# Expert tiles in float32: the expert's weights become the moving operand, the GELU outputs are turned for the second product, and the high and low parts go

## The reference, cut to what matters

```
h2 = layernorm(x) * g + b                      # 2048 x 192
logits = h2 @ gate_w + gate_b                  # 8 experts
wts, sel = top_k(logits, 2); wts = softmax(wts)
for e in range(8):
    he  = gelu(h2 @ w1[e] + b1[e])             # 192 -> 768
    res = res + cw[:, e:e+1] * (he @ w2[e] + b2[e])   # 768 -> 192
```

## Time and profile before

| what | value |
|---|---|
| median of three runs | 1736.37 us |
| the profiled execution: span from first to last instruction | 1779.8 us |
| TensorE busy with matmuls | 1403.7 us (79%) |
| VectorE, ScalarE, GpSimd busy | 890.2, 471.8, 238.8 us |
| mean granted TensorE clock | 0.703 of full |
| the expert tiles on TensorE, from the first transposes to the last product | 930.7 to 1139.4 us |

### The profile page before, as it was taken

One profiled execution on the slowest core, in us unless ns is written; L12 is line 12 of the kernel. 1 busy time (PEld: TensorE's weight loads), 2 busy tenths in 40 slices (PEclk: granted clock), 3 DMA queues, 4 the chain that ended last, 5 costly groups with the idle time before them and its releaser, 6 DMA issues.

```text
span 1779.8 us, 44781 instructions
## 1 busy us (share of the span) xinstructions
PE 1403.7 (79%) x19314; PEld 1194.5 (67%) x19314; DVE 890.2 (50%) x2335; ACT 471.8 (27%) x878; POOL 238.8 (13%) x248
## 2 busy tenths in 40 slices
PE   6888888897879999999639999616689999986251
PEld 5868776887657777777537777415689898985131
DVE  4444545445445464342523333345366666664876
ACT  1221122112224342241323333114113333313130
POOL 4100000004022000000160000252322222200000
PEclk9767877877679796595559999857555555555565
DMA  8000000012021000000131111110000000000001
GB/s 291 1 18 18 18 0 18 18 35 62 1 81 42 2 2 2 1 2 2 50 111 32 39 39 37 47 47 1 3 4 3 3 3 3 3 3 1 1 0 36
DMA packets 28771, 48.07 MB, mean 27 GB/s; under 512 B 3632, under 2 KB 21696, under 8 KB 28352
## 3 DMA queue, kind: packets, MB, share of 16 engines
q1 hardware_dynamic: 25536, 39.33, 7.4%
q0 software_dynamic: 3072, 6.30, 1.2%
HBM read 33.20 MB, written 12.41 MB: 26 GB/s over the span
## 4 chain that ended last, share of the span: by engine, by line
PE 62%; DVE 19%; POOL 10%; ACT 6%; issue 3%; DMA 0%; POOLq 0%; ACTq 0%; DVEq 0%
PE ps L1117 8%; PE ps L1229 6%; PE ps L831 6%; PE ps L941 4%; PE ps L897 4%; PE ps L1132 4%; DVE big L507 3%; DVE big L512 3%; POOL big L766 3%; POOL big L770 3%; PE ps L1003 2%; PE ps L966 2%; PE ps L851 2%; PE ps L525 2%; PE ps L1277 2%
## 5 line engine op out<-in xcount | busy, mean ns | idle before, releaser
L1229 PE MATMUL ps<-big 128*128 128x2 bf16 x7680 | 222.3, 165 | 43.8 <-POOL big L770 20.8
L1229 PEld LDWEIGHTS ps<-big 128*128 128x128 bf16 x7680 | 215.0, 104 | 56.4 <-DVE big L1994 23.8
L1117 PE MATMUL ps<-big 128*128 128x128 bf16 x1170 | 141.6, 218 | 1.0 <-DVE big L1910 0.5
L525 PE MATMUL ps<-ident,big 128*128 128x128 f32 x384 | 86.4, 411 | 66.7 <-ACT big L519 66.7
L1117 PEld LDWEIGHTS ps<-big 128*128 x1170 | 111.7, 96 | 27.3 <-issue 2.4
L525 PEld LDWEIGHTS ps<-ident,big 128*128 128x128 f32 x384 | 74.1, 217 | 82.5 <-ACT big L519 82.5
L831 PE MATMUL ps<-consts,big 96*128 96x192 f32 x512 | 111.3, 382 | 12.1 <-POOL iota L695 12.1
L831 PEld LDWEIGHTS ps<-consts,big 96*128 96x128 f32 x512 | 107.5, 260 | 12.9 <-issue 12.1
L1982 DVE TENSOR_REDUCE big<-ps 128x24 f32<-128x48 f32 x160 | 32.8, 205 | 142.3 <-PE ps L1229 141.7
L1917 DVE TENSOR_TENSOR big<-big 128x512 bf16<-128x512 f32 x78 | 41.5, 558 | 103.5 <-ACT big L1511 103.1
L507 DVE TENSOR_REDUCE big<-ps 128x3 f32<-128x768 f32 x64 | 58.1, 949 | 61.2 <-PE ps L881 61.2
(11 more groups left out here) (360 smaller groups left out, 2595.4 us busy)
## 6 DMA issues: line engine op xcount, KB each, us to landing
big<-x_dram SPq DMA_DIRECT2D x16, 384.0 KB, 3.4
consts<-packed_dram SPq DMA_DIRECT2D x1, 4459.0 KB, 17.8
rows_dram<-big SPq DMA_DIRECT2D x1, 3744.0 KB, 18.1
big<-rows_dram SPq DMA_DIRECT2D x39, 96.0 KB, 2.0
results_dram<-big SPq DMA_DIRECT2D x39, 96.0 KB, 1.6
big<-w_dram SPq DMA_DIRECT2D x12, 288.0 KB, 3.7
big<-w_dram SPq DMA_DIRECT2D x16, 192.0 KB, 4.0
big<-w_dram SPq DMA_DIRECT2D x4, 576.0 KB, 6.0
```

The lines of the kernel that those rows point to most:

```text
L525: last = nc.tensor.transpose(ps[s][:, k // 4, (k % 4) * P:(k % 4 + 1) * P], bufs[s].p[:, k * P:(k + 1) * P], ident[:, :])
L1117: last = nc.tensor.matmul(ps[0][:, 2 * (i % 2) + m // 4, m % 4 * P:(m % 4 + 1) * P], e_at(expert, at, P), side, start=(k == 0), stop=(k == ...
L1229: last = nc.tensor.matmul(sums[:, 2 * k:2 * k + 2], kernel_part(i, part)[:, at:at + P], x_parts[g % 4][:, k, 0:2], start=(part == 0), stop ...
```

## The change

The split is gone: tokens, weights and hidden values stay float32, and TensorE multiplies them as such.

- `m_turn(i)`: two float32 transposes, each of 96 columns of the rows, into partitions 0 to 95.
- `m_up(i)`: the turned tokens are now stationary (96 or 97 rows by 128; row 96 is a row of ones that brings in the bias), and the expert's weights, still named by a register, move: 512 and then 256 columns, two products each, four in all. The result has the tokens on the partitions. It has one buffer (two PSUM banks), not two.
- ScalarE applies GELU once. The hidden values must then be turned: `m_turn_hidden(i)`, six float32 transposes, and VectorE copies them out (`m_heT`), two copies.
- `m_down(i)`: six products, with the turned hidden values stationary and 192 columns of weights moving. VectorE copies the result (`m_y`) where it added halves before.
- TensorE's loop is one step deeper: turn tile i + 2, up of tile i + 1, turn the hidden values of tile i, down of tile i - 1.
- An expert is loaded straight into its place by two DMAs: three at the very start, three once the first values of the second attention are there (`f_xn`), two after its end (`f_out`). GpSimd, ScalarE and VectorE split nothing. SyncE's loop over the tiles is as it was.

```
-                for m in range(HT):
-                    for k, side in enumerate(sides):
-                        at = k * HIDDEN + m * P
-                        last = nc.tensor.matmul(ps[0][:, 2 * (i % 2) + m // 4, m % 4 * P:(m % 4 + 1) * P],
-                                                e_at(expert, at, P), side, start=(k == 0), stop=(k == CHUNKS - 1))
+                for half, cols in enumerate(m_halves):
+                    if i >= 1:
+                        pe.wait_ge(sem("m_gelu"), 2 * (i - 1) + half + 1)
+                    for c in range(2):
+                        rows = HC + 1 - c
+                        last = nc.tensor.matmul(m_hidden(half), e_x[i % 2][0:rows, c * P:(c + 1) * P],
+                                                e_at(expert, rows, c * HIDDEN + cols.start, cols.stop - cols.start),
+                                                start=(c == 0), stop=(c == 1))
+            def m_turn_hidden(i):
+                for half, cols in enumerate(m_halves):
+                    if i >= 1:
+                        pe.wait_ge(sem("m_heT"), 2 * (i - 1) + half + 1)
+                    pe.wait_ge(sem("m_gelu"), 2 * i + half + 1)
+                    for at in range(cols.start, cols.stop, P):
+                        last = nc.tensor.transpose(m_turned_hidden(half)[:, at - cols.start:at - cols.start + P],
+                                                   e_he[i % 2][:, at:at + P], ident[:, :])
+                    last.then_inc(sem("m_hidden_turned"), 1)
...
-                    for part, n in ((e_hi, 2 * C), (e_lo, C)):
-                        last = nc.tensor.matmul(o[:, 0:n], part[i % 2][:, cols], e_at(expert, at, n),
+                    last = nc.tensor.matmul(m_y_out(i), e_heT[i % 2][:, m * P:(m + 1) * P],
+                                            e_at(expert, P, 2 * HIDDEN + m * C, C), start=(m == 0), stop=(m == HT - 1))
...
-            for i in range(-1, TILES):
+            for i in range(-1, TILES + 1):
...
                 if 0 <= i and i + 2 < TILES:
                     m_turn(i + 2)
                 if i + 1 < TILES:
-                    m_up(i + 1, expert)
-                if 0 <= i:
-                    m_down(i, older)
+                    m_up(i + 1, experts[i + 1])
+                if 0 <= i < TILES:
+                    m_turn_hidden(i)
+                if 1 <= i:
+                    m_down(i - 1, experts.pop(i - 1))
...
+            for i in range(TILES + 1):
+                if i + 2 < TILES:
+                    m_x(i + 2)
+                if i < TILES:
+                    m_heT(i)
+                if 1 <= i:
+                    m_y(i - 1)
```

More of the change, by code:

```diff
@@ L301, in build, with e_at @@
         TILES = 2 * T // P + EXPERTS - 1
[L302 to L329, removed]
+        W_WORDS = 2 * HIDDEN + HT * C
+        W_AT = X3_AT - EXPERTS * W_WORDS
+        EARLY = tuple(range(EXPERTS - 1, 1, -1))
+        LATE = (1, 0)
+        assert f_used[0] <= W_AT + EARLY[-1] * W_WORDS
+        e_all = big[:, W_AT:X3_AT].rearrange("p (e n) -> p e n", e=EXPERTS)
+        e_bytes = big[:, W_AT:X3_AT].bitcast(U8).rearrange("p (e n) -> p e n", e=EXPERTS)
+        def e_at(expert, rows, at, n):
+            return e_bytes[0:rows, bass.ds(expert, 1), 4 * at:4 * (at + n)].rearrange("p o n -> p (o n)").bitcast(F32)
         IN_TOK = 3
@@ L371, in turned_back, with m_hidden, m_x_out, m_turned_hidden @@
             return ps[bank // 4][:, bank % 4, 0:2 * C].rearrange("p (s c) -> p s c", s=2)
+        m_halves = (slice(0, 4 * P), slice(4 * P, HIDDEN))
+        def m_hidden(half):
+            return ps[0][:, half, 0:(4 - 2 * half) * P]
+        def m_x_out(i):
+            return ps[0][0:HC, 2 + i % 2, 0:2 * P]
+        def m_turned_hidden(half):
+            return ps[1][:, half, 0:(4 - 2 * half) * P]
+        def m_y_out(i):
+            return ps[1][:, 2 + i % 2, 0:C]
         def stores(k):
@@ L597, in _ @@
                         "o p c n -> (o p) c n")).then_inc(sem(f"tok_x{s}"), 16)
[L599 to L612, removed]
-            sp.wait_ge(sem("b1_stored"), 16)
[L614 to L619, removed]
+            sp.wait_ge(sem("f_xn"), 1)
+            for e in EARLY[IN_TOK:]:
+                load_expert(e)
+            sp.wait_ge(sem("f_out"), U)
+            for e in LATE:
+                load_expert(e)
+            sp.wait_ge(sem("b1_kept"), 1)
+            sp.dma_start(b1s, b1_rows).then_inc(sem("b1_stored"), 16)
+            sp.wait_ge(sem("b1_stored"), 16)
+            sp.dma_start(e_all[HC:HC + 1, :, 0:HIDDEN],
+                         b1s.rearrange("(o e m) n -> o e (m n)", o=1, e=EXPERTS)).then_inc(sem("b1_loaded"), 16)
             def load_rows(i):
@@ L1102, in m_turn @@
                     pe.wait_ge(sem("m_x"), i - 1)
-                o = ps[1][:, i % 2, 0:ROW // 2].bitcast(BF16)
-                for c in range(3):
-                    last = nc.tensor.transpose(o[:, c * P:(c + 1) * P], e_row[i % 4][:, c * P:(c + 1) * P], identb[:, :])
+                for c in range(2):
+                    last = nc.tensor.transpose(m_x_out(i)[:, c * P:(c + 1) * P],
+                                               e_row[i % 4][:, c * HC:(c + 1) * HC], ident[:, :])
                 last.then_inc(sem("m_turned"), 1)
@@ L1498, in _ @@
                                  ACT.Copy).then_inc(sem("moe_cwT"), 1)
-            late_hi(1)
-            late_hi(2)
             def m_gelu(i):
                 if i >= 2:
-                    act.wait_ge(sem("m_down"), i - 1)
-                for half, cols in enumerate((slice(0, 4 * P), slice(4 * P, HIDDEN))):
+                    act.wait_ge(sem("m_hidden_turned"), 2 * (i - 1))
+                for half, cols in enumerate(m_halves):
                     act.wait_ge(sem("m_up"), 2 * i + half + 1)
-                    if i >= 2:
-                        act.wait_ge(sem("m_lo"), 2 * (i - 2) + half + 1)
-                    hidden = ps[0][:, 2 * (i % 2) + half, 0:cols.stop - cols.start]
-                    nc.scalar.activation(e_hi[i % 2][:, cols], hidden, ACT.Gelu)
-                    nc.scalar.activation(e_he[i % 2][:, cols], hidden, ACT.Gelu).then_inc(sem("m_gelu"), 1)
+                    nc.scalar.activation(e_he[i % 2][:, cols], m_hidden(half), ACT.Gelu).then_inc(sem("m_gelu"), 1)
             for i in range(TILES):
@@ L1840, in _ @@
             link(ins)
-            for j in range(4):
-                row_lo(j)
             def sums(k, by=0):
@@ L1857, in _ @@
             nc.vector.tensor_copy(place_i, place_f).then_inc(sem("m_places"), 1)
-            for j in range(4, 8):
-                row_lo(j)
             link(nc.vector.tensor_tensor(upto, sums(3).unsqueeze(1).to_broadcast([P, TILES, EXPERTS]),
```

162 lines of the change are left out of this document (39 added, 123 removed).

## The result

The changed kernel takes 1909.97 us, the median of four runs (1903.62 to 1916.75), against 1738.53 us before (four runs beside it). The ratio is 1.099, with a 95% interval of 1.095 to 1.104. The forecast was 1951 us and a ratio of 1.124, with the range 1860 to 2030: right in sign and within the range, 41 us too high. Some runs of a kernel come out longer as a whole, at a lower clock, and every ratio here leaves those out on both sides.

A forecast was written before the change was run, and what follows sets the result against it. TensorE was taken to set the pace of the expert tiles. Terms 41.7 + 105 + 70 + 4 - 5 - 0.7 gave +215 us, 1951 us on the median, ratio 1.124, range 1860 to 2030.

The forecast's parts named there:

- TensorE's work: Expert tiles: float32 work takes TensorE 6.42 us a tile against 5.35, over 39 tiles +41.7 us.
- the pause at 35 seams: Expert tiles: TensorE waits 3.0 us for rows requested behind the previous result, from tile 4 on, 35 times: +105 us.
- the clock that falls after it: Expert tiles: three pauses in four bring TensorE's lower clock, losing 2.65 us each: +70 us.
- filling: Start of the expert stage: it begins at the lower clock and the first GELU isn't covered: +4 us.
- earlier start: Before the scatter: no VectorE subtractions and quicker GpSimd indirect DMAs, -5 us; less VectorE waiting after splitting ends, -0.7.
- rivals 1 to 3: Expert tiles: clock holds despite pauses, 1881 us, chance 0.13; clock stays low throughout, 2131, 0.10; no pause, 1776, 0.06.
- Rival 4: Expert tiles: a float32 product costs one record, so not slower; 1650 us with no pause, chance 0.02.
- Costed at nothing: Two more experts loaded at the start, last two loads, ScalarE and VectorE work, single hidden buffer: no time added.

The follow-up runs named there:

- the filled pause: Changed kernel with 48 useless bf16 products ahead of each tile's row transposes from tile 4 on; 1863.72 us, ratio 1.072 to the kernel before.
- loading first: Changed kernel with SyncE asking for the rows of tile i + 4 ahead of the wait for result i; 1741.86 us, ratio 1.001 to before.
- the run of before with loads ahead: Kernel before the change, with SyncE asking for the rows of tile i + 4 ahead of the wait for result i; 1735.27 us, ratio 1.000.

## Why the prediction was right, and by how much not

The mechanism was the forecast one; one term was mis-sized. By the steps of the sum, in us:

| step | forecast | measured |
|---|---|---|
| TensorE's work, 39 tiles | +41.7 | +5.5 |
| the pause at 35 seams | +105 | +105 (99.5 idle, 5.6 draining) |
| the clock that falls after it | +70 | +58 by the lower stretches (28 x 1.7 + 3 x 3.4); the filled pause gave 46 back |
| filling | +4 | about +4, what is left of the stage's +171.9 |
| earlier start | -5.7 | -4.8 |
| sum | +215 | about +168; the medians differ by 171.4 |

- **TensorE's work** is the step that failed. I took it that each float32 instruction is recorded twice, from 384 records of L525 against 12 transposes for each of 16 images. The function runs for both halves of an image's softmax, so there are 24 an image, and a float32 transpose is one record; the earlier trace rows had it, with 12 records for one call of 12. Only float32 products have two. In the changed kernel L1079 has 234 records, 39 x 6, and L1089 has 468, 2 x 39 x 6. So the hidden values are turned in 0.65 us, not 1.31, and the rows in 0.26, not 0.44. The up product is 2.62 instead of 2.70, the 512-column record 0.43 and not 0.45. Together 5.49 us instead of 6.42, 36 us over the stage, the larger part of the 47 between the two sums. The clock's term, 12 us too high, is the rest.
- **The pause** was right in each of its links, and loading first takes all of it away.
- **The clock** was right in kind. Of the 35 seams with a pause 31 led to a fall, nearly nine in ten where I had put three in four; but 28 of these lose 1.7 us and three 3.4, not 2.65, as the lower level mostly lasted 3.4 us, shorter than most of the stretches I had read it from. The two errors partly cancel.
- **Earlier start.** From the last ranking product to the loads of rows it was 50.1 us before (878.50 to 928.63) and is 45.3 now (834.12 to 879.45). All 32 scatters but the first take 0.96 or 0.97 us.
- **The rivals.** The clock neither held nor stayed low throughout, and the pause came, so rivals 1 to 3 fall. With the loads first each tile has 8 transposes beside 20 records of products, and the clock stands at 1.00. The Trainium skill (TensorE: Matmul & The Clock Gate, Part 4: PE-mode transpose) has it that transposes do not engage the full clock; this trace shows no harm from them, though beside so many products it is no test of the rule by itself. Rival 4, the only one that was not slower, stood on the same miscount from the other side, but for products, where two records are real.
- **Costed at nothing.** The two experts more at the start did no harm that can be seen: TensorE begins the second attention at 496.7 us, against 504.7 in the profile of before and 494.5 in the run of before with loads ahead, and in the other runs of the changed tiles at 491.8 to 496.9. ScalarE and VectorE were busy for 18 and 31 of 100 us even without the pause.

## What to carry to other kernels

When a pipeline is made a step deeper, look at every request that stands behind its result, above all on a queue that computes nothing: the request moves with the result, its user doesn't. Ask for the next input when its buffer is free, not when an old output is done. And count the records of an operation against its own calls before a price is taken from them; here the loops around the call doubled it, and 36 of the forecast 215 us came from that.

## What the runs showed of the hardware that was not expected

- With a pause of 2.8 to 3.0 us in each tile the clock fell behind 31 of 35, and the tiles settled into one length: 28 of 37 intervals are 10.1 to 10.3 us, with one stretch of 3.4 us at the lower level in each. With 48 useless products, 2.7 us of work, in the pause the median was 8.5.
- With 1.8 to 2.0 us idle in each tile the clock held in the first tiles (but one) and the last, and fell in each of the 22 between. In the filled pauses it held over ten waits of 1.1 to 1.6 us and fell behind the one of 1.9. With 0.2 to 0.7 us (rows turned behind the up product) it stayed at 1.00.
- bf16 products of 128 columns whose stationary operand is named by a register follow each other at 0.112 us, the same number of bf16 columns turned at 0.056. With the same operand moving, ten products of 512 and 256 columns do the same arithmetic in 1.63 us instead of 3.7. That the naming is the cause is not shown. The trace of before lists an operation of TensorE's queue for each of the 1170 products, and as many loads of weights. The loads alone are not enough to explain it: the 1680 useless products of the filled pause have a load of weights each, too, from a fixed address, and follow each other at 0.056 us (48 in 2.84 us with the last one's draining).
